# A two-layer graph network on one Trainium2 core: three source batches instead of four before the sums move out, and a second buffer for the edge counts

## The reference

```
h = max(layernorm(x), 0)                                   # x: 6250 x 256
h_all[r] = h @ L0_weight[r].T                              # 8 relations
x = x + segment_sum(h_all[edge_type, src], dst) + L0_bias  # 206250 edges
h = max(layernorm(x), 0)
deg = segment_sum(1, [dst, loop]); dinv = rsqrt(deg)
out = segment_sum((dinv[src]*dinv[dst])[:, None] * (h @ W)[[src, loop]], [dst, loop]) + b
x = x + leaky_relu(out, 0.2)
```

## Time and profile before

| what | value |
|---|---|
| median of 3 runs | 2298.2 us (2296.88 to 2299.24) |
| the profiled execution | 2292.52 us, of which span 2290.7 us |
| busy: PE, ACT, POOL, DVE | 2002.0, 1608.2, 1639.5, 1221.0 us |
| stash loads | 19 |
| count loads | 156 |

### The profile page before, as it was taken

How to read it: one execution, slowest core, us unless ns; L and a number is a source line. 1 busy time by engine, 2 the same in 40 slices (tenths; PEclk the granted TensorE clock), 3 DMA queues, 4 the chain that set the end, 5 groups by cost and what they waited for, 6 DMA issues and landing times.

```text
span 2290.7 us, 44662 instructions
## 1 busy us (share of the span) xinstructions
PE 2002.0 (87%) x14354; PEld 1792.1 (78%) x14354; DVE 1221.0 (53%) x3510; ACT 1608.2 (70%) x3919; POOL 1639.5 (72%) x1740
## 2 busy tenths in 40 slices
PE   1467788788888898789899899999999999999897
PEld 1456677777788787778788789888888898988776
DVE  7446567657568666866756633223223232344267
ACT  4647677677878688778777877776767777676440
POOL 6577777777777777777777777777777777777414
PEclk9699998999999999999999999999999999999899
DMA  9435456556665665566665676655655555555465
GB/s 293 120 116 155 147 160 186 160 146 183 176 179 174 199 175 163 158 181 183 210 187 161 185 235 178 204 149 154 174 170 162 148 172 151 156 163 139 99 167 166
DMA packets 353088, 388.45 MB, mean 170 GB/s; under 512 B 217606, under 2 KB 273078, under 8 KB 352726
## 3 DMA queue, kind: packets, MB, share of 16 engines
q0 software_dynamic: 79072, 216.18, 32.7%
q1 hardware_dynamic: 228246, 124.11, 19.4%
q10 hardware_dynamic: 45536, 45.26, 5.9%
HBM read 307.65 MB, written 77.75 MB: 168 GB/s over the span
## 4 chain that ended last, share of the span: by engine, by line
PE 59%; POOL 17%; issue 7%; ACT 5%; DMA 4%; DVE 3%; ACTq 0%; DVEq 0%; SPq 0%; POOLq 0%
PE ps_slot L1601 20%; POOL rows_f L1101 15%; PE ps_slot L1661 13%; PE ps_proj L1617 12%; PE ps_aux L1661 9%; DMA rows_f<-table,idxT 3%; PE ps_slot L1631 3%; ACT staged_f L1277 1%; ACT wide_f L1333 1%; ACT gap_f L1340 1%; POOL recs_f L1089 1%; DMA abuf_f<-counts_d 1%; PE ps_slot L1680 1%; DVE hots_f L1497 1%; ACT acc_f L1263 1%
## 5 line engine op out<-in xcount | busy, mean ns | idle before, releaser
L1101 POOL DMA_INDIRECT rows_f<-table,idxT x1617 | 1534.3, 949 | 503.8 <-issue 473.4
L1601 PE MATMUL ps_slot<-onehot_f,rows_f 128*128 128x128 f32 x6468 | 864.8, 286 | 149.1 <-DMA rows_f<-table,idxT 120.3
L1601 PEld LDWEIGHTS ps_slot<-onehot_f,rows_f 128*128 128x128 f32 x6468 | 818.9, 199 | 184.1 <-DMA rows_f<-table,idxT 133.2
L1340 ACT ACTIVATE gap_f<-iota,keyT 128x128 bf16<-128x128 bf16 x1617 | 528.8, 395 | 77.0 <-ACT staged_f L1277 53.0
L1277 ACT ACTIVATE staged_f<-ps_slot 128x400 uint8<-128x400 f32 x800 | 345.4, 500 | 180.0 <-PE ps_slot L1631 179.7
L1494 DVE TENSOR_TENSOR hots_f<-ps_slot,keys_f 128x400 bf16<-128x400 bf16 x800 | 286.9, 359 | 297.3 <-PE ps_slot L1631 293.9
L1617 PE MATMUL ps_proj<-w0t,acc_f 128*128 128x256 f32 x1600 | 374.9, 389 | 0.0
L1348 ACT ACTIVATE onehot_f<-gap_f 128x384 f32<-128x384 bf16 x539 | 277.7, 515 | 100.5 <-PE ps_slot L1601 100.3
L1661 PE MATMUL ps_slot<-wide_f,stash_f 128*128 128x512 f32 (+1 forms) x1410 | 345.3, 390 | 0.9 <-ACT wide_f L1333 0.6
L1418 DVE TENSOR_TENSOR acc_f<-ps_slot,acc_f 128x256 f32 x539 | 228.0, 423 | 214.3 <-PE ps_slot L1601 147.6
L1617 PEld LDWEIGHTS ps_proj<-w0t,acc_f 128*128 128x128 f32 x1600 | 302.9, 194 | 44.9 <-issue 1.3
(11 more groups left out here) (156 smaller groups left out, 871.7 us busy)
## 6 DMA issues: line engine op xcount, KB each, us to landing
rows_f<-table,idxT POOLq DMA_INDIRECT x1617
abuf_f<-counts_d SPq DMA_DIRECT2D x66, 320.0 KB
stash_f<-table SPq DMA_DIRECT2D x15, 1280.0 KB, 9.0
table<-hs_f SPq DMA_DIRECT2D x50, 256.0 KB
keys_f<-counts_d SPq DMA_DIRECT2D x30, 320.0 KB
table<-xres SPq DMA_DIRECT2D x10, 640.0 KB, 6.7
acc_f<-x_d SPq DMA_DIRECT2D x50, 128.0 KB, 2.4
x_d<-xt_f SPq DMA_DIRECT2D x49, 128.0 KB
```

What stands on the lines that cost most here:

```text
L1101: eng.indirect_dma_start(rows0[:, k, c, :], None, V["table0"], bass.IndirectOffsetOnAxis(ap=idxT[:, n * LOT + c:n * LOT + c + 1], axis=0)) ...
L1340: last = eng.activation(gap[:, n % 2, c, :], iota[:, :], ACT.Abs, scale=-1.0, bias=V["key"][:, n * LOT + c:n * LOT + c + 1])
L1601: last = eng.matmul(o[:, b * W:(b + 1) * W], rows0[:, k, c, b * P:(b + 1) * P], onehot[:, n % HOTS, c, :], start=(c == 0), stop=(c == LOT ...
```

## The change

Three things differ in what the program does. `FIRST_BATCHES` is 3, so the sums of groups 0 to 5 leave after 18 units and not after 24. Counts have two buffers of their own, so that two, three and five are in use in the three phases, where it was one, two and four. And the planner's limit of pieces in one slot is 4 from `counts_end` on, where it was 2 until the tail. The functions `project_at` and `chain_at` give the slots that the constants gave before: `LATE_TILE` is 48 and the tiles to which they apply end at 47, so nothing moves by them.

```
-FIRST_BATCHES = 4
+FIRST_BATCHES = 3
-PROJECT_AT = (3, 7)
+LATE_TILE = 48
+def project_at(t):
+    return (t + 1) * LOTS + (1 if t >= LATE_TILE else 3), (t + 1) * LOTS + (3 if t >= LATE_TILE else 7)
+def chain_at(t):
+    base = (t + 1) * LOTS + (5 if t >= LATE_TILE else 9)
+    return base, base + 1, base + 2
-            while (half or todo) and pe + 1.2 <= limit and len(self.pieces.get(n, ())) < (2 if n < self.tail else 4):
+            while (half or todo) and pe + 1.2 <= limit and len(self.pieces.get(n, ())) < (2 if n < self.counts_end else 4):
-            allowed = 1 if n < self.counts_end + 4 else 2 if n < self.nlot + 4 else 4
+            allowed = 2 if n < self.counts_end + 4 else 3 if n < self.nlot + 4 else 5
-        abuf = sb("abuf", [P, UNIT], u8)
+        abuf = sb("abuf", [P, 2, UNIT], u8)
-        abufs = (abuf[:, :], keys[:, 0:UNIT // 2].bitcast(u8), spare[:, 0:UNIT], spare[:, UNIT:2 * UNIT])
+        abufs = (abuf[:, 0, :], abuf[:, 1, :], keys[:, 0:UNIT // 2].bitcast(u8), spare[:, 0:UNIT], spare[:, UNIT:2 * UNIT])
```

More of the change, by code:

```diff
@@ L720, in __init__ @@
             self.turn_win[b] = min(w for m, ws in self.win.items() if m + LEAD > n for w in ws)
-        stored = [end * LOTS + 18 for _, end in D.batch]
+        self.project = {n: (t, part) for t in range(D.tiles - 2) for part, n in enumerate(project_at(t))}
+        stored = [chain_at(end - 1)[2] + (5 if end > LATE_TILE else 7) for _, end in D.batch]
         stored[-1] = self.nlot + SEAM
@@ L730, in __init__ @@
             if n < self.nlot:
-                pe += 1.3 + 0.28 * len(self.win.get(n - LEAD, ())) + (3.45 if n >= LOTS and n % LOTS in PROJECT_AT else 0.0)
+                pe += 1.3 + 0.28 * len(self.win.get(n - LEAD, ())) + (3.45 if n in self.project else 0.0)
             elif n == self.nlot:
@@ L952, in both_layers @@
         s_cw = [sem(f"counts_out{i}") for i in range(2)]
-        s_ab = [sem(f"counts_in{i}") for i in range(4)]
+        s_ab = [sem(f"counts_in{i}") for i in range(5)]
         s_wide = sem("counts_widened")
@@ L1059, in chain_slots @@
         def chain_slots(t):
-            base = (t + 1) * LOTS + 9 if t < T - 2 else PL.nlot + 1 + 2 * (t - (T - 2))
+            if t < T - 2:
+                return chain_at(t)
+            base = PL.nlot + 1 + 2 * (t - (T - 2))
             return base, base + 1, base + 2
@@ L1697, in _ @@
                     sum_lot(n)
-                if n < PL.nlot and n >= LOTS and n % LOTS in PROJECT_AT:
-                    project(n // LOTS - 1, PROJECT_AT.index(n % LOTS))
+                if n in PL.project:
+                    project(*PL.project[n])
                 for t in (T - 2, T - 1):
```

6 lines of the change are left out of this document (3 added, 3 removed).

## The result

The changed kernel takes 2304.0 us in the median of 16 runs (2298.9 to 2306.5). The kernel before, measured again beside it, takes 2298.4 (2295.6 to 2302.9, 16 runs). The ratio is 1.0019, with a 95% interval of 1.0013 to 1.0026: slower by 4.4 us by the ratio (the two medians lie 5.6 us apart), where 10.3 were forecast. The direction holds and the time lies in the range; the size is less than half, and the ratio lies just inside the 0.2% that the prediction took as the edge of a measurable difference. The interval leaves out equality.

The account below looks back on a forecast made before the run. The prediction took POOL's train of gathers as the bound, with PE mattering only when the ring of seven lots is full. 11.5 - 1.3 + 1.5 - 1.4 = +10.3 us took the median from 2298.2 to 2308.5 us, range 2294 to 2319.

Parts of the forecast that it names:

- +11.5: Counting, about 906 to 1332 us: moved dense work that finds no room becomes POOL stall, +11.5 us; bounds 0 and +20.2.
- 26.1: PE time in us that 110 matmuls moved to slots 207 to 319 bring, at 2.37 us a piece of ten.
- 13.6: PE's waits from 906 to 1112 us for gathered rows (5.9) and DVE's accumulation (7.7), expected to vanish: 13.6 us.
- The return of 1: Counting: fewer idle gaps may raise PE's granted clock and return about 1 us.
- the others lie inside the counting, so I leave them: PE's waits from 906 to 1112 us for ACT's evacuation of counts and copy of keys, 10.7 + 2.2 us, held unchanged.
- +1.5 for switches of batch: Eleven more stash loads: half a 3.5 us ACT wait for counts at one of nine places, +1.5 us; bounds 0 and 31.5.
- -1.3 for the later stretch: Slots 440 to 457 freed: POOL can gain at most its real stall from 1348 to 2100 us, -1.3 us.
- -1.4 in the tail: Up to four pieces in slots 536 and 537 leave 8 matmuls fewer for the tail: -1.4 us.
- The faster one: Rival, 0.13: late counts cause the stall in the counting; the second counts buffer removes 10 us, giving 2285.5 us.
- Slower by more: Rival, 0.14: batch switches hold ACT up with the ring full, or waits inside the counting grow; 2322 us.
- No change: Rival, 0.15: all 28.0 us of PE idle time from 906 to 1112 us takes the moved work; 2297 us.
- Slower by over 0.2%: Chance of 0.69 that the changed kernel takes over 2302.8 us.

Follow-up runs that it names:

- Three batches alone: The kernel before with only the first phase cut from four batches to three, one counts buffer and the old piece limit kept; 1.0025, 2305.6 us.
- a deeper ring: The kernel before with a ring of eight lots for gathered rows instead of seven; ratio 0.9992 (0.9983 to 1.0001), stall 7.6 us.
- The thinned kernel: The changed kernel with dense pieces only in every third slot instead of every second, from slot 213 to 319; ratio 1.0048, 2307.8 us.
- the half pieces: The changed kernel with five matmuls a piece instead of ten (low part left out) in units first placed in slots 209 to 318; 0.9942, 2283.8 us.
- the changed kernel thinned from 264: The changed kernel with dense pieces only in every third slot from slot 264 to 319; ratio 1.0056, 2309.3 us.
- the buffer alone: The kernel before with only the second counts buffer, four batches and the old piece limit kept; ratio 0.9994, 2298.0 us.
- the repeat: The changed kernel run again unedited, against the kernel before; ratio 1.0022, 2302.6 us.
- the changed kernel with spread widenings: The changed kernel with ACT's widenings spread over up to three slots and counts loaded up to eight ahead; 0.9993 and 1.0040, the kernel before taking 2746.3 and 2772.2 us.

## Why the prediction came out as it did

**Direction and mechanism were right.** POOL's train of gathers sets the length; PE costs time only through a full ring. Freed work in slots 440 to 457 gave nothing, moved work in the counting cost stall. Three batches alone reproduce the effect, and a deeper ring takes 3.5 us of stall away, near a lot's worth. The prediction's signs of being wrong (stall at 10 us or less, waits for ACT gone by the double buffer, tens of us of waits for counts) did not come.

**The step that failed is the size of the first term, +11.5,** which measured +6.8: "11.5 us of work finds no room ... it becomes stall of POOL". It was 26.1 - 13.6 - 1, taken over into stall one for one. By the means of three profiles a side, two parts of it failed.

PE's stretch grew by 9.4 us and not by 11.5. The 26.1 measured 28.6, since 2.37 us was a piece at the higher clock. The 13.6 measured 13.6, in part by luck: it was read from half of the stretch in one profile, and over the whole of it (906 to 1348 us) the waits for rows and for DVE were 19.9, 21.3 and 26.6 us before and 9.0, 8.8 and 10.0 after. The return of 1 measured 4.5 in the sums and the projection, but not as a clock that is higher on the whole. And "the others lie inside the counting, so I leave them" cost 0.9.

The 9.4 us then became 6.8 of stall. PE's lag at lot 209 was less by 1.8 us in the changed group, which the prediction put at nothing. The six values run from 11.5 to 16.5 us, 11.5 and 14.2 in two profiles of the changed kernel and 16.5 and 14.2 in two of the kernel before, so it varies by execution; whether any of the 1.8 belongs to the change stays open. The profile that the prediction read was the one with the largest lag. The last 0.8 us are the other end of the stretch (0.2) and POOL's own pace (0.6).

The thinned kernel and the half pieces show why the waits inside the counting can't be held fixed. PE and ACT pace each other there, and when PE has less to do it waits more (29.3 us ahead of counts and keys' turns in the changed kernels, 45.7 in the thinned one, 46.3 with half pieces).

**+1.5 for switches of batch** measured nothing in the counting: ACT has no wait on a load of counts from 906 to 1348 us, and two afterwards (5.8 and 0.7 us), beside 6.8 before. Waits of that kind came in another plan, the changed kernel thinned from 264: 14.5 us of the 31.5 that the bound allowed.

**-1.3 for the later stretch** was a stall of one execution: two further profiles of the same work have 0.1. **-1.4 in the tail** did not show: +0.8 in the mean of three, and for the two profiles of the changed kernel alone, which have the limit of four pieces, 134.9 and 137.7 against 135.1, 136.6 and 137.0. These terms with the 6.8 come to 7.2 us, where the medians of the timed runs differ by 4.0 to 7.0; what lies between stays open.

**The stated marks.** Stall of 20 us or more: 17.0 to 18.4, not met. Its beginning before 1150 us: it begins at 1198 (1240 before), not met; at 1110 us the lag is 794/3 - 3108/12 = 5.7 lots against 6 forecast, and it stays at 5.7 at 1300. Waits for rows gone, waits for ACT not: met. At 1850 us the lag is 2.0 lots, not half of one, with 12.1 us of idle in 50 instead of 20. ACT's waits for counts under 5 us: met in the counting, 6.5 after it. The counts behind the lags, line 1115 (POOL) and then line 1615 (PE, PEld), to set beside the earlier trace rows:

```profile
0.00:1110.00 1110.00, 755.07 (x794) 0.93 0.61 181
0.00:1850.00 1850.00, 1298.98 (x1365) 0.95 0.61 182
```

```profile
0.00:1110.00 1110.00, 441.11 (x3108) 405.51 (x3108) 0.93 0.61 181
0.00:1850.00 1850.00, 741.39 (x5436) 697.49 (x5436) 0.95 0.61 182
```

**The rivals.** The faster one fell with the buffer alone at 0.9994. "Slower by more" did not happen to this change, though late loads of counts did appear in one of the other plans. "No change" named waits and the clock that gain by steadier work. The waits gained in part, the clock in sum did not, and some stall was added; the measured time lies between this rival's and the forecast. "Slower by over 0.2%", put at 0.69, did not come: 1.0019 lies within, if barely, and the repeat (1.0022) and three batches alone (1.0025) just outside.

## What to carry to other kernels

Find the engine whose train sets the length (here POOL, busy 72%) and price moved work by how full the buffer between it and the engine under change is at either place: freed PE time where the ring has room is worth nothing, added PE time near a full ring costs. Of work put into an idle engine, subtract the waits for upstream data, which vanish in part; treat waits that two engines cause each other as elastic in both directions. Before a half-per-cent difference is argued from two profiles, look at a duration that the change can't touch: the gathers' own time made 3.7 of the 9.9 us here. And read a term of a few us from several profiles: PE's elapsed time in the same stretch of the same work varied by up to 5.9 us.

## What the runs showed of the hardware

- The indirect gathers' median duration differs between executions of one kernel, 946 to 949 ns, with the issue gap of 0.30 us constant. POOL's busy time in all 1617 was 1533.3 and 1538.0 us in two executions of the changed kernel, 4.7 us apart.
- The changed kernel's PE ran at the higher clock (granted 1.00) until it had waited 2.1 us for rows before a sum that began at 1836.69 us; the granted clock fell to 0.50 at 1837.7, in that sum, and stood there to 1854.8 us, over waits of 1.74, 0.77 and 4.08 us. Twelve matmuls of a lot's sum took 2.93 us there, and 1.60 at 1854.92, also behind a wait (0.82 us), when the clock was back at 1.00. It is the clock of the moment, and not the wait itself, that the duration follows:

```profile
1851.20:1854.00 2.80, 2.80 (x12) 2.60 (x12) 0.00 (x0) 0.00 (x0) 1.97 (x3) 0.50 1.14 283
1854.90:1856.50 1.60, 1.58 (x13) 1.47 (x13) 0.00 (x0) 0.83 (x3) 1.02 (x2) 1.00 0.95 290
```

- Less dense work left PE longer at the lower clock: 38.7 us of the stretch from lot 209 to 319 in the changed kernels, 58.0 when thinned and 54.6 with half of the dense work left out. In the last the remaining sums and counts took 10.1 us longer than with all of it.
- In three sets of runs the kernel before took 2742 to 2772 us instead of 2298. The gathers were no slower in themselves (951 ns mean in the changed kernel with spread widenings), but POOL waited 277.1 us for something that the profile calls remote, and 255.1 us for PE. What that is, no run here tells.
